# Transposes of the identity at the ends of stages and ahead of the narrow and the joint attentions, in a four-layer decoder on one core

## The reference

```python
x = _layernorm(x + _L0_attn_ref(x, ...))        # 16 heads of 16
x = _layernorm(x + _L0_xattn_ref(x, ctx, ...))  # one head of 256
x = _layernorm(x + _L0_ffn_ref(x, ...))         # 8 experts, softmax affinity
x = _layernorm(x + _L1_attn_ref(x, ...))        # 16 heads of 16, alibi
x = _layernorm(x + _L1_xattn_ref(ctx, x, mask, ...))  # 4 heads, keys of both
x = _layernorm(x + _L1_ffn_ref(x, ...))         # 2 of 8 experts per batch
x = _layernorm(x + _L2_attn_ref(x, ...))        # 16 heads of 16, causal
x = _layernorm(x + _L2_xattn_ref(x, ctx, ...))  # 8 heads of 64
x = _layernorm(x + _L2_ffn_ref(x, ...))         # shared expert and truncated top 2
x = _layernorm(x + _L3_attn_ref(x, ...))        # 16 heads of 64, relative bias
x = _layernorm(x + _L3_xattn_ref(x, ctx, ...))  # 16 heads of 64
x = _layernorm(x + _L3_ffn_ref(x, ...))         # shared expert and top 2 of 8
```

## Time and profile before

| | us |
|---|---|
| median of 3 runs | 3615.69 |
| lowest, highest | 3615.62, 3618.03 |
| profiled execution, its own time | 3586.34 |
| span of the profiled execution | 3584.6 |
| TensorE busy | 3229.3 (90%) |
| VectorE busy | 1978.6 (55%) |
| ScalarE busy | 1656.0 (46%) |
| GpSimd busy | 1460.0 (41%) |
| mean granted clock of TensorE | 0.957 |

### The profile page before, as it was taken

How to read it: one execution, slowest core, us unless ns; L and a number is a source line. 1 busy time by engine, 2 the same in 40 slices (tenths; PEclk the granted TensorE clock), 3 DMA queues, 4 the chain that set the end, 5 groups by cost and what they waited for, 6 DMA issues and landing times. The chain is left out here.

```text
span 3584.6 us, 59373 instructions
## 1 busy us (share of the span) xinstructions
PE 3229.3 (90%) x23114; PEld 2587.5 (72%) x23125; DVE 1978.6 (55%) x4291; ACT 1656.0 (46%) x3866; POOL 1460.0 (41%) x1188
## 2 busy tenths in 40 slices
PE   6887999999698698599898898989998999989998
PEld 4566788888455355499555676868776888779997
DVE  5665222223565465477554564568776666656555
ACT  3554333332255354255355554345555655544554
POOL 2111434343210476277233443033333433328996
PEclk9999999999898799799899999999999999999999
DMA  1001100000000000243000101010000000015673
GB/s 62 2 10 53 42 18 19 36 1 1 22 2 2 22 1 1 89 165 142 27 3 2 44 6 48 1 50 35 1 1 31 9 6 4 1 71 180 218 224 104
DMA packets 53991, 157.29 MB, mean 44 GB/s; under 512 B 13522, under 2 KB 33378, under 8 KB 41300
## 3 DMA queue, kind: packets, MB, share of 16 engines
q1 hardware_dynamic: 49972, 143.26, 11.5%
q0 software_dynamic: 3744, 10.23, 1.0%
HBM read 142.42 MB, written 10.26 MB: 43 GB/s over the span
## 5 line engine op out<-in xcount | busy, mean ns | idle before, releaser
L1029 POOL TENSOR_TENSOR prob<-prob,inv 128x512 f32<-128x512 f32 x320 | 331.4, 1040 | 553.7 <-DVE inv L1070 548.8
L954 ACT ACTIVATE prob<-bank,nmax 128x256 f32<-128x256 f32 x640 | 297.3, 474 | 64.4 <-DVE nmax L1064 64.2
L2440 DVE TENSOR_TENSOR product<-bank,silu 128x512 f32<-128x512 f32 x128 | 88.6, 692 | 388.2 <-PE bank L2266 332.6
L2395 POOL TENSOR_TENSOR hL<-product,hH 128x512 fp32r<-128x512 f32 x128 | 165.4, 1293 | 321.5 <-ACT hH L2342 321.5
L1064 DVE TENSOR_REDUCE nmax<-bank 128x2 f32<-128x512 f32 x320 | 219.4, 687 | 91.2 <-PE bank L933 86.6
L2334 ACT ACTIVATE silu<-bank 128x512 f32<-128x512 f32 x128 | 76.5, 598 | 367.5 <-PE bank L2266 367.4
L1899 DVE TENSOR_REDUCE nmax<-bank 128x2 f32<-128x512 f32 x256 | 164.3, 683 | 106.6 <-PE bank L1485 106.6
L2266 PE MATMUL bank<-xH,upH 128*128 128x512 f32 x512 | 201.9, 394 | 6.2 <-POOL upL L2382 6.2
L2266 PE MATMUL bank<-xL,upH 128*128 128x512 f32 x512 | 201.4, 393 | 0.0
L2266 PE MATMUL bank<-xH,upL 128*128 128x512 f32 x512 | 199.7, 390 | 0.0
L890 PE MATMUL bank<-ident,prob 128*128 128x128 f32 x1280 | 168.7, 274 | 7.4 <-POOL prob L1029 7.3
(11 more groups left out here) (527 smaller groups left out, 10614.6 us busy)
## 6 DMA issues: line engine op xcount, KB each, us to landing
W<-in_L_ffn_experts SPq DMA_DIRECT2D x80, 1024.0 KB, 5.5
W<-in_L_ffn_experts SPq DMA_DIRECT2D x8, 1536.0 KB, 7.8
slots_y<-W SPq DMA_DIRECT2D x23, 256.0 KB, 6.1
W<-strips SPq DMA_DIRECT2D x4, 768.0 KB, 6.7
W<-in_L_ffn_experts SPq DMA_DIRECT2D x9, 256.0 KB, 4.5
X<-in_x SPq DMA_DIRECT2D x1, 2048.0 KB, 8.2
cs<-in_ctxT SPq DMA_DIRECT2D x16, 128.0 KB, 2.3
W<-in_L_ffn_experts SPq DMA_DIRECT2D x1, 2048.0 KB, 7.4
```

The lines of the kernel that those rows point to most:

```text
L954: ins = nc.scalar.activation(m_.prob[p % 2][:, e * 512 + j * S:e * 512 + (j + 1) * S], bank(key)[:, j * S:(j + 1) * S], ACT.Exp, bias=m_.n ...
L1029: nc.gpsimd.tensor_tensor(pr, pr, m_.inv[:, slot(p, e):slot(p, e) + 2].unsqueeze(2).to_broadcast([P, 2, S]), ALU.mult)\
L2395: nc.gpsimd.tensor_tensor(m_.hL[:, at], m_.product[s % 2][:, :], m_.hH[:, at].bitcast(F32), ALU.subtract).then_inc(g.h_low.sem, 1)
L2440: nc.vector.tensor_tensor(m_.product[s % 2][:, :], bank(("u", s))[:, :], m_.silu[s % 2][:, :], ALU.mult)\
```

## The change

A function `without_use` issues `count` transposes of the identity, of the identity as data, into the quarters of one bank, all without waits after the first; raises the bank's filled count; waits for it; and issues one more transpose that raises the freed count. Nothing reads the results. It is called behind all of TensorE's work of a block (late) or ahead of it (early):

| where | count |
|---|---|
| start of `attention16` (L0_attn, L1_attn, L2_attn), "early", bank 2 | 60 |
| start of `attention_both` (L1_xattn), "early", bank 0 | 90 |
| end of `attention16`, "late", bank 2 | 40 |
| end of `attention_both`, `attention64`, `experts_dense`, `experts_by_batch`, `experts_masked`, "late", bank 0 | 40 |

That is four early and ten late calls in the program: 670 transposes and 14 that follow them. `route` and `experts_sparse` have none, and nothing is added inside a stage.

```diff
+def without_use(nc, g, u, pe, key, count):
+    b = u.bank(key)
+    pe.wait_ge(g.freed[b].sem, u.before(key, 0))
+    for k in range(count):
+        mm = nc.tensor.transpose(g.psum[b][:, (k % 4) * P:(k % 4 + 1) * P], g.ident[:, :], g.ident[:, :])
+    mm.then_inc(g.filled[b].sem, 1)
+    pe.wait_ge(g.filled[b].sem, u.done(key, 0))
+    nc.tensor.transpose(g.psum[b][:, 0:P], g.ident[:, :], g.ident[:, :]).then_inc(g.freed[b].sem, 1)
```

```diff
@@ attention_both, the uses and TensorE's part
     u = g.uses()
+    u.add("early", 0)
...
+    u.add("late", 0)
...
+            without_use(nc, g, u, pe, "early", 90)
             wait_weights(pe, g, n)
...
+            without_use(nc, g, u, pe, "late", 40)
@@ attention16
+    u.add("early", 2)
...
+    u.add("late", 2)
...
+            without_use(nc, g, u, pe, "early", 60)
             wait_weights(pe, g, n)
             pe.wait_ge(g.scaled.sem, g.scaled.base + 1)
...
                 one_head(s)
+            without_use(nc, g, u, pe, "late", 40)
```

## The result

| | us |
|---|---|
| before, median of 8 runs | 3615.72 (3614.25 to 3627.12) |
| the change, median of 8 runs | 3606.22 (3601.41 to 3611.95) |
| ratio, 95% interval | 0.9972 (0.9961 to 0.9983) |
| forecast | 3606.5 (3594 to 3624) |

By the medians the change is 9.5 us faster, where 9.2 was forecast; the ratio of the runs says 0.28%. The sum was right; several of its terms were not, and that of L1_attn had the wrong sign.

The account below looks back on a forecast made before the run. TensorE bounds the middle of stages at full clock, while stage edges cost idle time and a half-clock stretch. Savings of 16.7 us less 7.3 and 0.2 of delays give 9.2 off the 3615.69 median: 3606.5 us, range 3594 to 3624.

Parts of the forecast that it names:

- that of L1_attn: Stage L1_attn: opening savings net of the held barrier at its end, forecast as 1.4 us shorter.
- Cost of a call: Each added transpose costs 0.109 us warm, 0.213 cold; a late call ends 4.8 to 4.9 us behind the last real matmul.
- Held barriers, 7.3 us: At stage ends, late calls outlast DVE and delay the barriers, 7.3 us in sum.
- L1_attn's was put at 1.7: End of L1_attn: its late call starts cold and delays the barrier by 0.5 to 4.8 us, taken as 1.7.
- Openings: Stage starts: work at full instead of half clock saves 16.7 us in sum, stage by stage.
- L3_ffn, put at 0: Opening of L3_ffn: no saving, 0 us, because POOL's split of the weights is last.
- Saved at an opening stays saved: After the openings, stages are TensorE-bound or run in fixed order at one pace, so all 16.7 us is kept.
- Identity doesn't count: Rival: transposes of the identity leave the clock at 0.50, giving 3660 us, slower by 1.2%; chance 0.05.
- The rule that I set beside it: Everywhere: transpose mode doesn't count as PE-busy the same way, so the change brings no clock and only its costs.
- The held barrier outweighs the clock: Rival: seven barriers wait for the late calls while only 2.1 us comes back, giving 3624 us; chance 0.10.
- Bound by others: Rival: POOL and DMA bound the openings, so 7.8 us saved meets 7.5 lost, 3615 us, no change; chance 0.20.
- The 29 us between the timed runs and the profiled one: Whole program: timed runs stand 29 us above the profiled execution, cause unknown; carried over unchanged into the forecast.

Follow-up runs that it names:

- late_24: The change with 24 instead of 40 transposes in each late call; 3579.99 us against 3590.73 before, ratio 0.9969.
- change_timed: The change again without edit, timed beside its early calls alone and late calls alone, for a third profile; 3581.85 us, ratio to before 0.9975.
- after_again: The change again without edit, for a second profile; 3592.02 us in one run.
- before_again: The kernel before, without edit, for a second profile; 3590.70 us, where before was 3590.73 on this chip.
- gaps_24: The change with late calls of 24 and four more calls in remaining waits (95, 100, 50, 24 transposes); 3580.89 us against 3593.23 before, ratio 0.9957.
- early_only: The change with its four early calls and no late call; 3577.33 us against 3593.23 before, ratio 0.9954.
- late_only: The change with its ten late calls of 40 and no early call; 3599.28 us, ratio to before 1.0019.
- shift_three: The change with 90 instead of 60 transposes in L1_attn's early call; 3610.56 us in one run.
- no_late_l0ffn: The change without the late call at the end of L0_ffn; 3608.55 us in one run.
- shift_half: The change with 66 instead of 60 transposes in L1_attn's early call; 3611.73 us in one run, before 3618.83.
- picked: The change with late calls of 24 at the ends of L0_attn, L1_xattn, L2_xattn only, plus 50 in experts_dense and 95 in route; 3595.91 us against 3618.83, ratio 0.9934.

## Why the prediction was right, point by point

*Cost of a call.* Right: 0.109 us each, 4.8 us to the end of a late call, 8.90 for 80. A call that begins cold costs more: L1_attn's early one took 8.6 us for 7.1, still inside its 9.0.

*Held barriers, 7.3 us.* The tails of the first profile give 1.0, 0.8, 0.4, 1.0, 1.2, 0.4, 1.2 and 0.4: 6.4 us. L1_attn's was put at 1.7 and is 0.8, since the clock rose during the call. late_24 shows that it can be had back, at the price of some of the clock in L0_ffn, L2_xattn and L3_ffn.

*Openings.* To the 128th real matmul, from the first profile of before to change_timed: L1_attn 3.3 (3.1 forecast), L2_attn 3.1 (3.1), L0_attn 1.3 (1.1), L2_ffn 2.4 (2.0), L0_ffn 0.9 (0.6), L1_xattn 4.5 in this profile and 0.9 to 1.0 in the two others (3.2); route 1.2 (0.6). L2_attn's is 1.5 in after_again, and L0_attn's would be 4.1 against before_again. So 3.2 for L1_xattn was right in one profile of three: the sum took it that the 90 transposes reach to the first real work, and the context's DMA decides that, as shown above. L2_xattn 0.6 and L3_xattn 0.5 were forecast at 1.2 each: they begin warm, but lose the clock in their waits for POOL. L3_attn was put at 0.6 and lost 0.8 (0.1 lost and 0.4 won in the two others).

*L3_ffn, put at 0.* Wrong, +3.2. The step that failed is the 0 behind "POOL's split of the weights is last". POOL is last: TensorE's start of the gate products is as late as before, 6.9 us from the barrier. But the transposes finish sooner, and the wait grows from 1.02 to 3.08 us:

```profile
3170.31 3.69 PE L2960 MATMUL bank<-ident,X 128*128 128x128 f32 x32 [0.32 <-PEq L818]
3177.08 0.40 PE L2970 MATMUL bank<-xH,gateH 128*8 128x512 f32 x1 [3.08 <-POOL gateL L3141]
```

In it the clock falls, and the gate products run at 0.56, where before has 1.00 from 3178.4 on. This loses 1.6 us. In gaps_24 the 32 transposes are as fast as in the change (3.69 us), 24 more fill the wait, and the 1.6 us is back; late_24 has it back with nothing in the wait, since its transposes are slower (5.35 us) and leave a wait of 1.41. The other half is open: early_only, late_24 and gaps_24 open L3_ffn like before and still took 414.5 us for 412.0, with a slow stretch at 25 us that is 6.8 us long for 3.4, and one more at 62 us.

*"Saved at an opening stays saved."* This step failed. It holds where TensorE is full, as in the 250 us window of the earlier trace rows: from the 600th to the 2900th matmul of L3_ffn no time is won or lost between before and the change. The narrow attentions end in a long drain in which the clock falls and comes back, and there the alignment of the work decides: L1_attn won 3.3 us at its opening, lost 0.8 at its barrier and 6.7 in its drain, L2_attn ranged from 262.1 to 268.9 us in profiles with either opening. That L1_attn's loss and L3_ffn's were made up by 3.3 more in L1_xattn and 4.8 more in L2_attn is chance, not the forecast's merit: these are the two stages that differ most from one profile of the change to the next.

*Rivals.* "Identity doesn't count" fell: the start of the program shows 60 in 8.31 us. The rule that I set beside it, of the Trainium skill, TensorE: Matmul & The Clock Gate, Part 4: PE-mode transpose, doesn't agree with this case: by it the early calls would have stayed at 0.213 each and come to 12.8 us. "The held barrier outweighs the clock" is true of the late calls by themselves (late_only, 1.0019) and not of the change, whose early calls lie ahead of work in the chain. "Bound by others" holds for L2_xattn and L3_xattn; L1_ffn gained 0.7 us, where 0.5 of loss was forecast, by the 1.2 us that route keeps. The 29 us between the timed runs and the profiled one were the chip's, most likely in L3_ffn, so that taking them over unchanged was right.

## What to carry to other kernels

Idle transposes pay ahead of a stage's first work, inside a wait that another engine sets, and only as many as fit: four early calls brought 0.46%, and every one too many at a barrier cost its full 0.109 us. A wait that ends with a DMA varies from one execution to the next, and a count that just fits it holds the clock in some of them only; a call that starts cold needs more room, 10.1 us for 60 in L2_attn where 7.1 do when it starts warm. Take an opening's worth from whether TensorE's work there is in the chain, and look for the wait behind it: an opening made faster makes that wait longer, and the clock may fall in it instead. A stage that drains with the clock at its edge can move by 5 to 8 us for a shift of a few tenths, and here that, not the held barriers, is most of what the late calls cost; compare stage by stage, in several profiles, before a gain or loss there is put down to an edit.

## What was not expected of the hardware

- L1_attn's last third held 0.50 for 54.6 us in the change and for 34.2 in early_only, with its real work in the same places within 0.1 us up to the fall. What the clock goes by there isn't settled; shift_three and no_late_l0ffn show that moving the work changes it, shift_half that 0.15 us the wrong way doesn't.
- The stage L3_ffn took 25 us more on some chips: in the first profile of the change all of it is lost between 364 and 421 us of the stage, where TensorE stands in 15 waits of 14.0 us together for which the profile names no releaser. Their cause wasn't tried.
- Products with 8 columns depend on the clock nearly as much as wide ones: 32 in 6.97 us at 0.50, and in 3.86 at 0.94 in picked.
